# Transposed scores by query tile over four heads, three PSUM banks per kind of score, one visit per key tile to the values

## The chip, the cores and the metric

The kernel runs on one NeuronCore of a Trainium2 chip. The metric is the device time of one execution in microseconds, as the median of several runs. Engines are named as the profile names them: PE (TensorE, with its weight loads shown apart as PEld), DVE (VectorE), ACT (ScalarE), POOL (GpSimd) and SP (SyncE, which here only issues DMAs).

## The reference, cut to what matters

```python
x = L0_attn_x                                   # (2, 2048, 1024) float32
xn = layernorm(x)
q = (xn @ wq).reshape(b, s, 32, 32)             # 32 query heads of 32
k = (xn @ wk).reshape(b, s, 8, 32)              # 8 key heads, each serves 4 query heads
v = (xn @ wv).reshape(b, s, 8, 32)
scores = where(causal, q @ k.T / sqrt(32), min)
s = (softmax(scores) @ v).reshape(b, s, 1024) @ wo
base = xn @ W_base.T + b_base
g = silu(base + lora_out)                       # rank-16 experts, top 2 of 8 by a router
out = x + s * g
```

## The kernel before

The program has four stages that follow one another: `project` (layer norm, q, k, v, router), `attend`, `gate` (base and lora, silu) and `output` (wo and the residual). The change is in `attend`, and in the few constants that are made for it at the start of the program.

`attend` works on 16 groups (2 batches of 8 key heads). A group has four query heads that share one key head. Its 2048 queries are cut in 4 chunks of 512 (`c` = 0 to 3), and a chunk sees 4(c+1) key tiles of 128 keys (`j`). Four kinds of work run on PE, interleaved by a fixed order (`stage`), and the text calls them by the letters of that order:

- **S**, row scores (L747): for one query tile `i`, one head `h` and one piece of 512 keys `p`, queries lie on the partitions. DVE takes the maximum over the keys (L905). There are 160 pieces in a group, 64 of them on the diagonal, 128 to 512 keys wide, and each of these 64 gets a second matmul that adds a causal mask (L750). Four PSUM banks (`rows_ps`) hold them. The pieces are computed 72 ahead of T (`LEAD`), partly for the next group.
- **M**: when a chunk has all its maxima, `shift` is formed (L911), turned by PE (L756), copied by DVE (L915) and carried by a DMA into one more row of `q_st` (L675), so that T subtracts the maximum by itself.
- **T**, transposed scores (L804): for one key tile `j` and one head `h`, keys lie on the partitions and up to 512 queries on the columns. Two banks (`cols_ps`) hold them. On the diagonal a T is 512, 384, 256 or 128 wide and gets a mask matmul of 128 columns (L807). ACT takes the exponential into `probs`, one of four buffers, by key tile (L887). A group has 160 T, 64 of them on the diagonal.
- **V** (L821) and **L** (L831): the exponentials times the values, and times ones (the row sums), into `o_ps` and `l_ps`, four heads side by side in the columns of PE. V runs for all 40 key tiles of a group, L for 17. The exponentials of the other 23 are first added up by POOL (L737), 20 additions in a group, and one L for each of chunks 1 to 3 takes that sum at the chunk's end (**Y**, L841).

A step is one key tile: four T, each followed by one S. A V stands after the second pair and an L, where there is one, after the fourth. When a chunk is done, ACT copies `l_ps` and `o_ps` out (**O**, L896 and L897), DVE takes the reciprocal of the sums in eight slices of 128x64 between the S of the next chunk (L949), multiplies (L956), and SP stores the result. 14 of the 16 groups run in a loop whose body is two groups; it turns between chunk 0 and chunk 1.

## Time and profile before

| | |
|---|---|
| median of 3 runs | 3855.75 us (3852.77 to 3857.87) |
| span of the profiled execution | 3855.3 us |
| first S of `attend` on PE | 666.7 us |
| first T | 703.0 us |
| last matmul of `attend` | about 3078 us |
| first matmul of `gate` | 3094.9 us |
| mean granted TensorE clock | 0.981 of full speed |

From the first T to the last matmul of `attend` are 2375 us, 16 groups. The profile is read by stretches: a table of busy time by stretch gives what each engine does in one group, and the timeline of a few microseconds shows the matmuls with their start times. A matmul's duration contains its way through the array, so two that follow each other overlap in the records; what one costs PE is the distance from its start to the next start, not its duration. "Idle before" on PEld names what the weight load waited for.

### The profile page before, as it was taken

To read this page: it belongs to the slowest core of one execution; us is meant where nothing else is said; L and a number is where in the kernel's file an instruction comes from. 1 tells how busy PE (TensorE), PEld (TensorE's weight loads), DVE (VectorE), ACT (ScalarE), POOL (GpSimd) and SP (SyncE) were. 2 spreads that over 40 slices of the span, in tenths; PEclk is the share of its full clock that TensorE was granted. 3 is DMA by queue.
4 is the path that set the end of the run, shared out by engine and by line. 5 is a ranking of instruction groups with operands and counts; after the bars stand their busy time and mean duration, and the time that the engine had idled before them with its cause. 6 is when DMAs were issued, how large, how long until landed. Compare 5 with 4: busy or idle time off the path is not lost. (4 is left out here: it accounts for less than half of the span.)

```text
span 3855.3 us, 66009 instructions
## 1 busy us (share of the span) xinstructions
PE 3712.1 (96%) x21376; PEld 2272.1 (59%) x21376; DVE 2212.6 (57%) x4099; ACT 1557.0 (40%) x3042; POOL 1379.6 (36%) x349
## 2 busy tenths in 40 slices
PE   7999998999999999999999999999999889998999
PEld 6888886544444444444444444444444378887887
DVE  5343332877777777777777677777777322222333
ACT  3122210455555555555555555555555511011000
POOL 0000000465565574565465565555655600000000
PEclk9999998799999999999999999999999999999999
DMA  6555444211101102101101111111010054444555
GB/s 219 167 175 159 153 145 146 79 34 35 46 20 49 38 23 48 39 26 45 43 26 45 37 32 42 35 35 45 21 47 18 6 179 145 137 137 162 191 189 174
DMA packets 232906, 326.87 MB, mean 85 GB/s; under 512 B 16800, under 2 KB 132512, under 8 KB 231072
## 3 DMA queue, kind: packets, MB, share of 16 engines
q1 hardware_dynamic: 229008, 310.48, 26.7%
q10 hardware_dynamic: 3600, 12.58, 1.0%
q8 instruction: 167, 2.74, 0.3%
q14 instruction: 131, 1.07, 0.1%
HBM read 188.25 MB, written 134.22 MB: 84 GB/s over the span
## 5 line engine op out<-in xcount | busy, mean ns | idle before, releaser
L905 DVE TENSOR_REDUCE neg_max<-rows_ps 128x1 f32<-128x512 f32 (+3 forms) x2560 | 1434.3, 602 | 600.7 <-PE rows_ps L747 427.2
L887 ACT ACTIVATE probs<-cols_ps 128x512 f32<-128x512 f32 (+3 forms) x2560 | 1270.4, 533 | 1059.4 <-PE cols_ps L804 542.9
L737 POOL TENSOR_TENSOR added_pool<-added_pool,probs 128x2048 f32<-128x2048 f32 (+2 forms) x272 | 1137.0, 4180 | 296.6 <-ACT probs L887 285.5
L804 PE MATMUL cols_ps<-q_st,k_st 97*128 97x512 f32 (+3 forms) x2560 | 1089.6, 428 | 61.7 <-ACT probs L887 42.9
L747 PE MATMUL rows_ps<-k_st,q_st 96*128 96x512 f32 (+3 forms) x2560 | 1021.7, 405 | 16.9 <-DMA q_st<-scratch_q_hi 16.9
L804 PEld LDWEIGHTS cols_ps<-q_st,k_st 97*128 97x128 f32 x2560 | 488.2, 191 | 820.6 <-ACT probs L887 702.8
L821 PE MATMUL o_ps<-probs,v_st 128*32 128x512 f32 (+3 forms) x5120 | 605.7, 545 | 0.0
L747 PEld LDWEIGHTS rows_ps<-k_st,q_st 96*128 96x128 f32 x2560 | 510.6, 200 | 40.9 <-issue 17.1
L737 POOL TENSOR_TENSOR added_pool<-probs 128x2048 f32<-128x2048 f32 x48 | 219.5, 4573 | 726.3 <-ACT probs L887 726.3
L949 DVE RECIPROCAL l_raw<-l_raw 128x64 f32<-128x64 f32 x512 | 275.3, 540 | 56.2 <-ACT a_o_raw L897 56.2
L438 PE MATMUL acc<-xt_hi,w_hi 128*128 128x512 f32 x704 | 281.6, 400 | 0.6 <-DVE logits L381 0.6
L440 PE MATMUL acc<-xt_hi,w_lo 128*128 128x512 f32 x704 | 277.6, 394 | 0.0
L439 PE MATMUL acc<-xt_lo,w_hi 128*128 128x512 f32 x704 | 276.8, 393 | 0.0
L720 POOL TENSOR_TENSOR gw_lo<-gw_raw,gw_hi 128x1024 fp32r<-128x1024 f32 x9 | 21.0, 2372 | 672.3 <-ACT gw_hi L862 672.3
L750 PE MATMUL rows_ps<-mask_ij,ident_b 128*128 128x128 bf16 x1024 | 241.8, 236 | 0.0
L395 DVE SCALAR_TENSOR_TENSOR out_lo<-acc,out_hi 128x512 fp32r<-128x512 f32 x80 | 55.3, 692 | 324.4 <-ACT out_hi L290 324.4
L1082 PE MATMUL g_acc<-gw_hi,g_t_hi 128*128 128x512 f32 x576 | 225.2, 391 | 16.9 <-DMA g_t_lo<-scratch_hw_lo 16.9
L807 PE MATMUL cols_ps<-mask_ji,ident_b 128*128 128x128 bf16 x1024 | 237.9, 232 | 0.0
L831 PE MATMUL l_ps<-probs,ones 128*32 128x512 f32 (+3 forms) x2176 | 228.0, 491 | 0.0
L1083 PE MATMUL g_acc<-gw_lo,g_t_hi 128*128 128x512 f32 x576 | 224.9, 390 | 0.0
L1084 PE MATMUL g_acc<-gw_hi,g_t_lo 128*128 128x512 f32 x576 | 224.8, 390 | 0.0
L1202 PE MATMUL o_acc<-ow_hi,o_t_hi 128*128 128x512 f32 x512 | 200.4, 391 | 11.2 <-DVE o_t_lo L1168 11.2
(101 smaller groups left out, 3155.0 us busy)
## 6 DMA issues: line engine op xcount, KB each, us to landing
q_st<-scratch_q_hi SPq DMA_DIRECT2D x128, 256.0 KB, 4.4
x_sb<-in_x SPq DMA_DIRECT2D x32, 512.0 KB, 4.0
scratch_xt_hi<-xt_hi SPq DMA_DIRECT2D x32, 512.0 KB, 6.0
scratch_xt_lo<-xt_lo SPq DMA_DIRECT2D x32, 512.0 KB, 6.8
scratch_q_hi<-out_hi SPq DMA_DIRECT2D x64, 256.0 KB, 2.4
scratch_q_lo<-out_lo SPq DMA_DIRECT2D x64, 256.0 KB, 2.9
q_st<-scratch_q_lo SPq DMA_DIRECT2D x64, 256.0 KB, 4.6
scratch_o<-o_sb SPq DMA_DIRECT2D x64, 256.0 KB, 2.4
```

Source lines behind the costliest of these rows:

```text
L438: nc.tensor.matmul(out, lh, rh, start=(k == 0), stop=False)
L439: nc.tensor.matmul(out, lh, rl, start=False, stop=False)
L440: ins = nc.tensor.matmul(out, ll, rh, start=False, stop=(k == KT - 1))
L737: nc.gpsimd.tensor_tensor(added["pool"][:, :, q0:CH], a[:, :, q0:CH], probs[j % 4][:, :, q0:CH], ALU.add).then_inc(pool_added, 1)
L747: ins = nc.tensor.matmul(out[:, 0:keys], q_st[c][0:K1, h, i * P:(i + 1) * P], k_st[kbuf][0:K1, CH * p:CH * p + keys], start=True, stop=p < c)
L750: ins = nc.tensor.matmul(out[:, keys - P:keys], ident_b[:, :], mask_ij[:, :], start=False, stop=True)
L804: ins = nc.tensor.matmul(cols_ps[h % NCOLS][:, q0:CH], k_st[u][:, j * P:(j + 1) * P], q_st[c][:, h, q0:CH], start=True, stop=not diagonal)
L807: ins = nc.tensor.matmul(cols_ps[h % NCOLS][:, q0:q0 + P], ident_b[:, :], mask_ji[:, :], start=False, stop=True)
L821: ins = nc.tensor.matmul(o_ps[h * HD:(h + 1) * HD, q0:CH], v_st[vbuf][:, j, :], probs[j % 4][:, h, q0:CH], start=(j == 0), stop=(j == step ...
L887: nc.scalar.activation(probs[j % 4][:, h, q0:CH], cols_ps[h % NCOLS][:, q0:CH], ACT.Exp) \
L905: nc.vector.tensor_reduce(neg_max[chunk % 2][:, r, p:p + 1], rows_ps[bank % NROWS][:, 0:keys], AX.X, ALU.max, negate=True).then_inc(rows_f ...
L949: ins = nc.vector.reciprocal(l_raw[cp % 2][:, part], l_raw[cp % 2][:, part])
```

## The change

- **T by query tile.** One T is now one key tile `j` and one query tile `i` over all four heads: 4 x 128 = 512 columns, always. A group has 136 T, of which 16 are on the diagonal; each of these gets a mask matmul of 512 columns (`ident_r`, `mask_ji` in fp32r). ACT writes the exponentials of a T to four places of `probs`.
- **Banks.** Three `rows_ps` (were four), three `cols_ps` (were two); `probs` has five buffers (were four); `gw_raw` two (were four).
- **Row masks on DVE.** The 64 diagonal S of a group have no mask matmul. Their maximum is taken by `tensor_tensor_reduce`: the bank plus a constant `tri` in SBUF, written to `masked_rows` in bf16, with the maximum as accumulated result. In the program this is two DVE instructions, the second on 128x1.
- **One visit.** V and L of a key tile stand together (`weigh`), after the third T behind the key tile's last T. L runs for 16 key tiles, POOL makes 21 additions in a group. Y stands with the last visit of a chunk.
- **Order.** The S are spread evenly: 164 S and M over 136 T, 84 ahead. M comes after three S of the next chunk (was two). O stands two T behind a chunk's last visit.
- **Reciprocals.** The row sums are no longer inverted as 128x512. A DMA gathers one row of each head as 128x16 (L1), DVE inverts that in one instruction (I), a DMA stores it (L2), four DMAs read it back spread over the partitions (L3), DVE multiplies (N), a DMA stores the result (L4). I, L2, L3, N and L4 stand 8, 9, 13, 18 and 19 T behind the last visit of the chunk.
- The loop turns between chunks 1 and 2.

```diff
-LEAD = 72
-TURN_AFTER = 2
-NROWS, NCOLS = 4, 2
+TURN_AFTER = 3
+NROWS, NCOLS, NPROBS = 3, 3, 5
+LEAD = 84
+VISIT_AFTER = 3
+def tiles_of(c):
+    return [(j, i) for j in range(TPC * (c + 1)) for i in range(max(0, j - TPC * c), TPC)]
...
-ADDS = {"pool": [[], [0, 1, 3, 4, 6], [0, 1, 3, 4, 6, 7, 9, 10], [0, 1, 3, 4, 6, 7, 9, 10, 12, 13]]}
+ADDS = [[], [0, 1, 2, 4, 5], [0, 1, 2, 4, 5, 6, 8, 9], [0, 1, 2, 4, 5, 6, 8, 9, 10, 12, 13]]
...
+        _t = tiles_through(_c, _j) + VISIT_AFTER - 1
+        event(_t, "W", _c, _j)
+    event(_t + 2, "O", _c)
+    event(_t + 4, "L1", _c)
+    event(_t + 8, "I", _c)
+    event(_t + 9, "L2", _c)
+    event(_t + 13, "L3", _c)
+    event(_t + 18, "N", _c)
+    event(_t + 19, "L4", _c)
...
-                if p == c:
-                    ins = nc.tensor.matmul(out[:, keys - P:keys], ident_b[:, :], mask_ij[:, :], start=False, stop=True)
...
+                keys = keys_of(c, i, p)
+                wait_apart(dve, rows_full, full, passed_rows)
+                nc.vector.tensor_tensor_reduce(masked_rows[rows_slot(k)][:, 0:keys], bank[:, 0:keys], tri[:, CH - keys:CH],
+                                               1.0, MASKED, ALU.add, ALU.max, into).then_inc(rows_free, 1)
...
-                        ins = nc.tensor.matmul(cols_ps[h % NCOLS][:, q0:CH], k_st[u][:, j * P:(j + 1) * P], q_st[c][:, h, q0:CH],
-                                               start=True, stop=not diagonal)
+                        ins = nc.tensor.matmul(into, k_st[n.u][:, j * P:(j + 1) * P], q_st[c][:, :, i * P:(i + 1) * P],
+                                               start=True, stop=not diagonal)
+                        if diagonal:
+                            ins = nc.tensor.matmul(into, ident_r[:, :], mask_ji[:, :, :], start=False, stop=True)
...
-                        ins = nc.vector.reciprocal(l_raw[cp % 2][:, part], l_raw[cp % 2][:, part])
+                        nc.vector.reciprocal(l_inv[cc % 2][:, :], l_few[cc % 2][:, :]).then_inc(l_inv_ready, 1)
```

First place, PE in chunk 3, key tiles below the diagonal (`cols_ps` is T, `rows_ps` is S or M, `o_ps` is V, `l_ps` is L or Y). Before, from one T to behind the next V:

```order
L804 MATMUL cols_ps0<-q_st3,k_st0 128x512
L747 MATMUL rows_ps3<-k_st1,q_st1 128x512
L804 MATMUL cols_ps1<-q_st3,k_st0 128x512
L747 MATMUL rows_ps0<-k_st1,q_st1 128x128
L750 MATMUL rows_ps0<-mask_ij,ident_b 128x128
L804 MATMUL cols_ps0<-q_st3,k_st0 128x512
L747 MATMUL rows_ps1<-k_st1,q_st1 128x512
L821 MATMUL o_ps<-probs1,v_st0 32x512 x4
```

The same place now, with the last visit of chunk 2 in it:

```order
L895 MATMUL cols_ps2<-q_st3,k_st0 128x512
L818 MATMUL rows_ps1<-k_st1,q_st0 128x512
L855 MATMUL o_ps<-probs3,v_st0 32x128 x4
L860 MATMUL l_ps<-probs3,ones 32x128 x4
L867 MATMUL l_ps<-added,ones 32x512 x4
L895 MATMUL cols_ps0<-q_st3,k_st0 128x512
L818 MATMUL rows_ps2<-k_st1,q_st1 128x512
L895 MATMUL cols_ps1<-q_st3,k_st0 128x512
L818 MATMUL rows_ps0<-k_st1,q_st1 128x128
L818 MATMUL rows_ps1<-k_st1,q_st1 128x512
L895 MATMUL cols_ps2<-q_st3,k_st0 128x512
L824 MATMUL rows_ps2<-ident,shift 16x128
```

The T rotate over three banks, an S has no mask behind it, some T are followed by two S, and V, L and Y stand in one block.

Second place, PE on the diagonal of chunk 1. Before:

```order
L831 MATMUL l_ps<-probs2,ones 32x512 x4
L804 MATMUL cols_ps0<-q_st1,k_st1 128x384
L807 MATMUL cols_ps0<-mask_ji,ident_b 128x128
L747 MATMUL rows_ps3<-k_st1,q_st3 128x512
L804 MATMUL cols_ps1<-q_st1,k_st1 128x384
L807 MATMUL cols_ps1<-mask_ji,ident_b 128x128
L747 MATMUL rows_ps0<-k_st1,q_st3 128x512
L821 MATMUL o_ps<-probs3,v_st1 32x512 x4
```

Now:

```order
L895 MATMUL cols_ps0<-q_st1,k_st1 128x512
L898 MATMUL cols_ps0<-mask_ji,ident_r 128x512
L818 MATMUL rows_ps0<-k_st1,q_st3 128x512
L895 MATMUL cols_ps1<-q_st1,k_st1 128x512
L818 MATMUL rows_ps1<-k_st1,q_st3 128x512
L895 MATMUL cols_ps2<-q_st1,k_st1 128x512
L818 MATMUL rows_ps2<-k_st1,q_st3 128x512
L855 MATMUL o_ps<-probs3,v_st1 32x512 x4
```

Where each narrow T had a mask, one full T in a key tile has one.

Third place, DVE at the end of a chunk's normalisation (`rows_ps` into `neg_max` or `row_max` is the maximum of an S). Before:

```order
L905 TENSOR_REDUCE neg_max1<-rows_ps1 128x1
L905 TENSOR_REDUCE neg_max1<-rows_ps2 128x1
L949 RECIPROCAL l_raw0<-l_raw0 128x64
L905 TENSOR_REDUCE neg_max1<-rows_ps3 128x1
L905 TENSOR_REDUCE neg_max1<-rows_ps0 128x1
L949 RECIPROCAL l_raw0<-l_raw0 128x64
L956 TENSOR_TENSOR o_sb0<-a_o_raw0,l_raw0 128x512
```

Now, in chunk 1, where the N of the group before's chunk 3 meets the I of chunk 0:

```order
L960 TENSOR_REDUCE row_max1<-rows_ps0 128x1
L1007 RECIPROCAL l_inv0<-l_few0 128x16
L1011 TENSOR_TENSOR o_sb1<-o_sb1,l_all1 128x512
L960 TENSOR_REDUCE row_max1<-rows_ps1 128x1
L960 TENSOR_REDUCE row_max1<-rows_ps2 128x1
L964 ISA masked_rows0,row_max1<-rows_ps0,tri 128x128
L964 ISA row_max1 128x1
```

Eight slices became one small instruction, a diagonal maximum became two instructions, and the multiplication comes earlier in the chunk than before.

## Rows read from the trace of the kernel before

**Rows 1.** The page, part 1 (PE) and part 2 (granted clock).

```profile
PE 3712.1 (96%) x21376; PEld 2272.1 (59%) x21376; DVE 2212.6 (57%) x4099; ACT 1557.0 (40%) x3042; POOL 1379.6 (36%) x349
...
PEclk9999998799999999999999999999999999999999
```

**Rows 2.** Busy time by stretch, two stretches of one group; columns in the first line.

```profile
core 0: us, PE busy (x) PEld busy (x) DVE busy (x) ACT busy (x) POOL busy (x), PEclk, DMA share, GB/s
...
1440.60:1587.60 147.00, 143.95 (x936) 69.45 (x932) 109.80 (x204) 82.60 (x168) 84.81 (x21) 1.00 0.15 37
1587.62:1739.52 151.90, 146.65 (x937) 70.72 (x933) 109.96 (x204) 82.93 (x168) 84.77 (x21) 0.98 0.14 36
```

**Rows 3.** Timeline of PE in chunk 3: start, duration, work, [idle before].

```profile
1700.48 0.50 PE L804 MATMUL cols_ps<-q_st,k_st 97*128 97x512 f32 x1
...
1701.66 0.19 PEld L804 LDWEIGHTS cols_ps<-q_st,k_st 97*128 97x128 f32 x1 [0.21 <-ACT probs L887]
...
1703.77 0.50 PE L804 MATMUL cols_ps<-q_st,k_st 97*128 97x512 f32 x1
...
1704.10 0.40 PE L747 MATMUL rows_ps<-k_st,q_st 96*128 96x512 f32 x1
...
1704.34 0.40 PE L804 MATMUL cols_ps<-q_st,k_st 97*128 97x512 f32 x1
...
1704.58 0.28 PE L747 MATMUL rows_ps<-k_st,q_st 96*128 96x256 f32 x1
...
1704.71 0.23 PE L750 MATMUL rows_ps<-mask_ij,ident_b 128*128 128x128 bf16 x1
...
1704.87 1.07 PE L831 MATMUL l_ps<-probs,ones 128*32 128x512 f32 x8
...
1705.86 0.19 PEld L804 LDWEIGHTS cols_ps<-q_st,k_st 97*128 97x128 f32 x1 [0.84 <-ACT probs L887]
```

**Rows 4.** Timeline around the copies of O.

```profile
1468.91 0.60 ACT L897 ACTIVATE a_o_raw<-o_ps 128x512 f32<-128x512 f32 x1
...
1470.06 0.50 PE L804 MATMUL cols_ps<-q_st,k_st 97*128 97x512 f32 x1 [0.67 <-ACT probs L887]
```

**Rows 5.** Groups by line and form, 800 to 3000 us: count, busy us, mean ns.

```profile
L905 DVE TENSOR_REDUCE neg_max<-rows_ps 128x1 f32<-128x512 f32 x1664 | 1081.4, 681 | 455.4 <-PE rows_ps L747 405.3 <-PE rows_ps L750 34.3 <-issue 5.4
...
L737 POOL TENSOR_TENSOR added_pool<-added_pool,probs 128x2048 f32<-128x2048 f32 x193 | 882.1, 4571 | 211.4 <-ACT probs L887 203.9
...
L949 DVE RECIPROCAL l_raw<-l_raw 128x64 f32<-128x64 f32 x479 | 259.3, 541 | 0.0
```

**Rows 6.** Timeline of DVE and POOL where a multiplication meets an addition.

```profile
1506.39 9.24 POOL L737 TENSOR_TENSOR added_pool<-added_pool,probs 128x2048 f32<-128x2048 f32 x2 [2.11 <-ACT probs L887]
...
1514.62 1.56 DVE L956 TENSOR_TENSOR o_sb<-a_o_raw,l_raw 128x512 f32<-128x512 f32 x1
```

**Rows 7.** Timeline of the diagonal: an S behind a T's mask.

```profile
1606.28 0.48 PE L747 MATMUL rows_ps<-k_st,q_st 96*128 96x512 f32 x1
...
1606.60 0.22 PE L804 MATMUL cols_ps<-q_st,k_st 97*128 97x128 f32 x1
...
1606.70 0.47 PE L747 MATMUL rows_ps<-k_st,q_st 96*128 96x512 f32 x1
```

**Rows 8.** Timeline where the loop turns.

```profile
1612.10 0.79 PE L804 MATMUL cols_ps<-q_st,k_st 97*128 97x512 f32 x1 [2.19 <-issue]
```

**Rows 9.** Timeline: first S of `attend`, first matmul of `gate`.

```profile
666.71 0.45 PE L747 MATMUL rows_ps<-k_st,q_st 96*128 96x128 f32 x1 [16.93 <-DMA q_st<-scratch_q_hi]
...
3094.86 0.79 PE L1082 MATMUL g_acc<-gw_hi,g_t_hi 128*128 128x512 f32 x1 [16.87 <-DMA g_t_lo<-scratch_hw_lo]
```

**Rows 10.** One line's instructions (T): count, ns min/median/max, first and last start.

```profile
L804 PE MATMUL cols_ps<-q_st,k_st x2560: 223/421/796, 703.0 to 3075.3; 97*128 97x512 f32 x139, 97*128 97x384 f32 x20, 97*128 97x128 f32 x19, 97*128 97x256 f32 x19
```

**Rows 11.** The page: a DVE form that reads a bank and SBUF.

```profile
L395 DVE SCALAR_TENSOR_TENSOR out_lo<-acc,out_hi 128x512 fp32r<-128x512 f32 x80 | 55.3, 692 | 324.4 <-ACT out_hi L290 324.4
```

**Rows 12.** DMA issues: the shortest, median us to landing.

```profile
q_st<-row SPq DMA_DIRECT2D x64, 8.0 KB, 1.8
```

More of the change, by code:

```diff
@@ new lines, with tiles_through, cols_slot, before_in @@
+NSG = len(ROWS)
+TILES = [(c, j, i) for c in range(CPB) for j, i in tiles_of(c)]
+NTG = len(TILES)
+T_OFF = [sum(len(tiles_of(cc)) for cc in range(c)) for c in range(CPB + 1)]
+J_OFF = [TPC * c * (c + 1) // 2 for c in range(CPB + 1)]
+NJG = J_OFF[CPB]
+NVG = NJG
+LEAD = 84
+VISIT_AFTER = 3
+assert NJG % NPROBS == 0
+def tiles_through(c, j):
+    return T_OFF[c] + sum(1 for t in tiles_of(c) if t[0] <= j)
+def cols_slot(t):
+    return 1 if t == NTG - 1 else t % NCOLS
+def before_in(slot_of, count, t):
+    return next(p for p in range(t - 1, -count, -1) if slot_of(p % count) == slot_of(t))
@@ L542, in stage @@
     return order
 STAGES = [stage(c) for c in range(CPB)]
-def before(op):
-    return op[0] in ("O", "I", "N") or op[-1] == "before"
-def first_uses():
-    out = []
-    for i in range(LEAD):
-        out.append(("S", *piece_at(i)))
-        if i >= TURN_AFTER and piece_at(i - TURN_AFTER)[2]:
-            out.append(("M", *piece_at(i - TURN_AFTER)[:2]))
-    return out
-FIRST_USES = first_uses()
-USES = [sum(op[0] in "SM" for op in st) for st in STAGES]
-NSG = sum(USES)
-S_OFF = [len(FIRST_USES) + sum(USES[:c]) for c in range(CPB)]
@@ L566, with of_group_before, of_group_after @@
[L566 to L581 removed]
+def of_group_before(op):
+    return op[0] not in "TSM" and op[2] == 1
+def of_group_after(op):
+    return op[0] in "SM" and op[3] == 1
@@ L583, in attend, with adds_through @@
+FIRST_ROWS = [k for k in range(LEAD) if ROWS[k] != ("M", CPB - 1)]
+ADDS = [[], [0, 1, 2, 4, 5], [0, 1, 2, 4, 5, 6, 8, 9], [0, 1, 2, 4, 5, 6, 8, 9, 10, 12, 13]]
+NADD = sum(len(a) - 1 for a in ADDS if a)
+def adds_through(c, j):
+    return sum(max(0, len(a) - 1) for a in ADDS[:c]) + sum(1 for t in ADDS[c][1:] if t <= j)
+def attend(nc, sc, ident, ident_r, mask_ji, tri, wb, lb, gw_hi, gw_lo):
     ctx = ExitStack()
@@ L774, in run @@
+            def run(n, c, ops):
                 for op in ops:
                     kind = op[0]
-                    if kind in "VLY":
-                        old = op[-1] == "before"
-                        cc = (c - 1) % CPB if old else c
-                        back = 1 if old and c == 0 else 0
-                        steps = TPC * (cc + 1)
-                        to_sum = [j for j in range(steps) if not any(j in ADDS[who][cc] for who in ADDS)]
-                        adders = [who for who in ADDS if ADDS[who][cc]]
@@ L920, in _ @@
             ins.then_inc(ones_ready, 1)
[L921 to L933 removed]
+            dve.sem_inc(rows_free, 1)
@@ L934, in run @@
+            for k in FIRST_ROWS:
+                count = rows_count(None, 0, k)
+                if ROWS[k][0] == "S":
+                    _, chunk, last, piece = ROWS[k]
+                    piece_max(count, k, chunk, *piece)
+                    if last:
+                        shifts(chunk, count)
+                else:
+                    row_out(count, k, ROWS[k][1] % 2)
+            def run(n, c, ops):
                 for op in ops:
                     kind = op[0]
-                    at = S_OFF[c] + use
```

506 lines of the change are left out of this document (263 added, 243 removed).

## Prediction

> **What bounds the kernel now.** I read the page first: PE is busy 96% of the span, at nearly full granted clock, and no other engine is over 57% [rows 1]. A busy PE may still be waiting, because a matmul's record holds its way through the array, so I went on to the stretches. A group of `attend` takes 147.0 us, and there DVE is busy 109.8, ACT 82.6 and POOL 84.8 us; none of them sets the pace by its sum [rows 2]. Then the timeline of PE. At the 2.4 GHz level a full S or T starts 0.24 us after the one before it (1704.10, 1704.34, 1704.58). A V or L takes 0.99 us until the next T's start (1704.87 to 1705.86), and the S behind that T comes after 0.33 us instead of 0.24, because the T's weight load was not hidden. Two T and two S with a block take 2.09 us (1703.77 to 1705.86), all of it PE's own work. Two T and two S without a block take 1.18 us (1700.48 to 1701.66), and 0.21 of these are a wait for ACT, which has not emptied the second bank [rows 3]. Behind the two copies of O the next T waits 0.67 us and the step loses about 1.25 us [rows 4]. So PE's own work is about 137 of the 147 us, and ACT's banks cost the other 10. That work, and then the waits, are where the change acts. `project`, `gate` and `output` keep their code.
>
> **The change part by part**, in us for each group.
>
> T and their masks. Both kernels stream 136 x 512 columns for T, but before in 160 starts and 64 masks. An S behind a mask takes 0.32 instead of 0.24, and a 128 wide T with its mask takes 0.10 on top (1606.28, 1606.60, 1606.70) [rows 7]; a mask therefore costs about 0.12. The 64 diagonal T average 0.16, so with masks 64 x 0.28 = 17.9. Now 40 full T and 16 full masks at 0.24: 13.4. Some narrow T hide their load better than I assume; I take -3.5, bounds -1 and -5.
>
> Row masks leave PE. Where an S stands before a V or L, the mask is absorbed: 1704.58 to 1704.71 to 1704.87 is hardly more than the array needs to drain. Elsewhere it costs the 0.12 of above. About a third of the S stand before a block: 64 x 0.08 = -5, bounds 0 and -8.
>
> One visit. Of 17 L, 6 already stood right behind a V. The other 11 each cost an entry and an exit: 0.99 less the 0.85 of four passes over 512 columns is 0.14, then 0.09 for the exposed load and some 0.14 to drain the S before it, 0.37 in all: -4. The L now cover 896 columns fewer in four passes, -1.5. Together -5.5.
>
> Bank waits on T. 80 pairs of T less 51 blocks and the 4 with O leave 25 halves at 0.21: -5. With three banks and 136 exponentials of 0.55 to 0.6 (80 us in a group) ACT has no deficit to hand on: by the time a visit starts, the exponential it needs has been waited for by a T. O: the copies stand two T behind a visit and take 1.2; V of the next chunk's first tile stands two T later, about 1.0 us, and needs them. The T behind wait about 0.75 where they waited 1.25: 4 x -0.5 = -2.
>
> DVE. 96 plain maxima go back to back at 0.55 to 0.6, as now. The diagonal ones are a form that the trace lacks; the nearest row, one bank and one SBUF input, takes 0.69 for 512 [rows 11], where the plain one takes 0.68 [rows 5], so 0.49 for the mean width of 320, and the second instruction adds about 0.15. Reciprocals shrink from 32 x 0.54 = 17 [rows 5] to 4 small ones. The sum is 96 x 0.57 + 64 x 0.64 + about 10 = 106 of some 132: not the bound, but with three banks instead of four its bursts now reach PE. The Trainium skill gives such a two-input fp32 operation (N + 151) / 0.96 ns ("VectorE: DVE Perf Modes", The TRN2 errata), 0.49 us for 320; by that page the sum stays as it is.
>
> The multiplication N has both inputs in SBUF, and the trace shows what it does beside POOL: it starts at 1514.62, POOL's addition ends at 1515.63, and it ends at 1516.18, 0.55 later [rows 6]. It waits for the whole addition. In the new order N of chunk 3 falls 10 T into chunk 1, about 7.5 us in, inside POOL's first addition (about 6.5 to 11.1). DVE is away some 4 us, PE has three banks of S, about 2 us: a stall of 2. The other three fall near an addition's end, 0.5 together. The chain of I needs the copies plus one DMA of about 1.8 [rows 12], 5 us; 6 T and two visits lie between, so it just arrives. Adding 0.08 for each of 40 visits for the third bank I take +6, bounds 0 and +16.
>
> POOL. 18 full and 3 narrower additions are 18 x 4.57 + 3 x 3.45 = 93 [rows 5]. They begin when a chunk's second tile is ready, and Y waits for the last. In chunk 3 that is 6.5 + 44.6 + 1.8 (a gap before tile 4) = 53, where Y stands at about 53 too. Over the group this floor is about 125. So POOL's cover of Y is just used up; any further gain on PE would end there.
>
> Sum: 147 - 3.5 - 5 - 5.5 - 5 - 2 + 6 = 132 us for a group, -15; over 16 groups -240.
>
> Once per run. The turns of the loop cost about 5 us each, 2.19 of it at the first T [rows 8], and stay. The distance from the first T to the last, 2372 [rows 10], is 16 x 147 + 7 x 5 less 15, part of which the last group owes to having no S; now POOL holds that group back, +5. Before the first T stand 36 us of S (666.7 to 703.0) [rows 9, 10]; 9 more S and one bank fewer, at the 1.2 GHz level, +10. The loading of `gate`'s weights through two buffers ends before that. At the end four DMA hops of about 2 replace 3.5 us of reciprocals: +6. Constants at the start: +2. Together +23.
>
> 3855.3 - 240 + 23 = 3638 as a span. The median of the runs shown is 0.45 above the profiled span, so 3639.
>
> **The rivals.**
>
> POOL's floor (A). If masks and blocks were worth their upper bounds and DVE did not disturb, PE alone would need about 121, and Y would hold the group at 125: 3855 - 352 + 23 = 3526. For it: PE in the profile has no other releaser than ACT. Against: three `rows_ps` and a loaded DVE.
>
> DVE as bound (B). If the new form runs at two cycles an element, a diagonal maximum costs 1.0 instead of 0.64 and DVE needs 96 x 0.57 + 64 x 1.0 + 10 = 129, in bursts; a group ends at about 139: 3855 - 128 + 23 = 3750. For it: the form is not in the trace and is two instructions. Against: [rows 11].
>
> Slower (C): the diagonal maximum waits for POOL as N does. It reads `tri` from SBUF, 64 times a group, while POOL is busy 93 us. A wait that meets POOL at random costs half an addition, 2.3 us, in a share 93/G of the cases: G = 132 + 64 x 2.3 x 93/G gives G = 200, so 3855 + 53 x 16 + 23 = 4726. It decides from about 0.25 us of unhidden wait for each diagonal maximum. For it: [rows 6] show the lock with certainty, for two SBUF inputs. Against: in the new form one input is a bank; no row has such a form while POOL works. The Trainium skill says a DVE instruction with at most one SBUF input outside the two-port modes does not contend with GpSimd ("SBUF — State Buffer", Who interferes with whom). By that rule C is out and 3639 stands, without it the time is that of C; the lock on N, by the same section, agrees with the trace.
>
> Nothing gained (D): the long matmul masks, the fetch of the longer DVE program or a late DMA in the chain L1 to L3 (N would hold DVE, then PE) eat the 15 us, about 3.8 us in each chunk: 3855 + 23, with the additions once per run, 3878 at the point where all is eaten. For it: SP's queue holds L3 of one chunk before L1 of the next, and DVE stands in order at I and N. Against: the distances above, which leave some 4 us for each hop of about 2.
>
> **How the numbers follow.** The forecast, 3560 to 3720, has 0.63; A 0.11; B 0.15; C 0.05; D 0.06, most of it slower. The range takes in A and B with their own widths: 3525 to 3790. The bounds of the terms give 147 - 1 - 0 - 5.5 - 5 - 2 + 16 = 149 on one side if all fall badly at once, and POOL's floor on the other; I take no more than half of the bad side. A measurement of this kernel can tell about 0.2% from no change. Faster 0.89, within 0.2% 0.01, slower 0.10.
>
> **What would show it.** In the profile after: a group of about 132 us between two turns of the loop; PEld of T no longer waiting for ACT except behind O; new waits of PE for DVE (`row_max`), the longest beside the multiplication of chunk 3; ISA records of the diagonal maxima of about 0.49 plus 0.15; Y waiting little or not for POOL; POOL busy about 93 of 132. If the diagonal maxima show durations of up to an addition, it is C. If DVE is busy over 95% of a group, it is B. If Y waits for POOL in each chunk, it is A. Waits for a DMA at the reciprocal or the multiplication mean D.

## The result: 3913 us, slower by 1.5%

The changed kernel takes 3913.16 us (median of 4 runs, 3910.23 to 3920.0), the kernel before 3856.69 beside it. The ratio is 1.0149, with a 95% interval of 1.0135 to 1.0163. The forecast was 3639, range 3525 to 3790: sign and range were both wrong.

The page of the changed kernel, part 1, and from part 2 the row of the granted clock:

```profile
PE 3604.7 (92%) x19072; PEld 2230.1 (57%) x19072; DVE 2143.2 (55%) x4677; ACT 1491.2 (38%) x2658; POOL 1527.9 (39%) x366
...
PEclk9999998898999899999999989999999989999999
```

Beside [rows 1] PE has 107 us less work in a span that is 53 us longer, and the clock is no longer at 9 in every slice of `attend`. A group, from one Y of chunk 2 to the same Y of the next group, and the next one, which has a turn of the loop in it; the columns are those of [rows 2]:

```profile
1407.16:1557.01 149.85, 136.91 (x796) 66.86 (x789) 105.69 (x241) 78.58 (x144) 93.98 (x21) 0.94 0.17 45
1557.01:1710.89 153.88, 139.83 (x797) 67.94 (x789) 105.53 (x241) 78.99 (x144) 93.97 (x21) 0.92 0.17 43
```

So a group takes 149.85 us where the forecast said 132. PE is busy for 136.9 of them, but part of that time at a lower clock (0.94 in the mean). Part 5 of the page, two of the rows that differ most from before: S (L818) and the multiplication N (L1011).

```profile
L818 PE MATMUL rows_ps<-k_st,q_st 96*128 96x512 f32 (+3 forms) x2560 | 987.1, 410 | 182.9 <-DVE row_max L960 118.2
...
L1011 DVE TENSOR_TENSOR o_sb<-o_sb,l_all 128x512 f32<-128x512 f32 x64 | 234.2, 3659 | 10.0 <-DMA l_all<-scratch_l_inv 10.0
```

N is an instruction of 0.69 us when nothing disturbs it, and takes 3659 ns on average here. In the kernel before, S waited for no maximum. Now PE is idle for 182.9 us in front of it, 118.2 of them until a maximum (L960) has freed a bank. The waits between 900 and 2700 us (engine, line, releaser: us in total, times, longest):

```profile
PEld cols_ps L895 <- ACT probs L939: 231.0, 304, 1.2
...
PE rows_ps L818 <- DVE row_max L960: 85.6, 36, 3.0
...
PE rows_ps L818 <- DVE row_max L964: 33.8, 12, 2.8
...
PEld l_ps L867 <- POOL added L801: 0.3, 2, 0.2
```

PE waits 119.4 us for DVE in 48 stalls of 2.5 us each: four in each group, one for each N. Y hardly waits for POOL (0.3 us), and T's weight loads wait 231 us for ACT where they waited 528.3 with two banks.

**Where N stands.** The timeline of DVE and POOL in one group, the rows of N in chunk 1 and of the additions next to them:

```profile
1484.20 4.56 POOL L801 TENSOR_TENSOR added<-probs 128x2048 f32<-128x2048 f32 x1 [19.23 <-ACT probs L939]
...
1486.89 2.43 DVE L1011 TENSOR_TENSOR o_sb<-o_sb,l_all 128x512 f32<-128x512 f32 x1
...
1488.85 4.88 POOL L801 TENSOR_TENSOR added<-added,probs 128x2048 f32<-128x2048 f32 x1
...
1497.34 8.41 POOL L801 TENSOR_TENSOR added<-added,probs 128x2048 f32<-128x2048 f32 x2 [3.61 <-ACT probs L939]
...
1498.37 4.07 DVE L1011 TENSOR_TENSOR o_sb<-o_sb,l_all 128x512 f32<-128x512 f32 x1
```

The first N starts 2.69 us into an addition and ends 0.56 us behind its end (1489.32 less 1488.76), as in [rows 6]. The second starts 1.0 us into an addition, waits for the rest of it, and takes 4.07. The N of the next two chunks start at 1529.74 and 1574.51, 0.7 and 1.2 us behind the start of an addition (1529.01, 1573.34), and take 4.37 and 3.92.

**What PE does meanwhile.** Its timeline at the second N: an S of chunk 1 finds all three banks full, waits, and what follows is slower.

```profile
1497.66 0.40 PE L818 MATMUL rows_ps<-k_st,q_st 96*128 96x512 f32 x1
1497.90 0.40 PE L895 MATMUL cols_ps<-q_st,k_st 97*128 97x512 f32 x1
...
1503.09 0.79 PE L818 MATMUL rows_ps<-k_st,q_st 96*128 96x512 f32 x1 [2.79 <-DVE row_max L960]
1503.68 0.63 PE L895 MATMUL cols_ps<-q_st,k_st 97*128 97x512 f32 x1
1504.11 0.63 PE L818 MATMUL rows_ps<-k_st,q_st 96*128 96x512 f32 x1
```

Ahead of the stall two full matmuls start 0.24 us apart, behind it 0.43. That is the 1.2 GHz level. Busy time in the 7 us behind each of the four stalls of this group, from the stall's end (the granted clock is the third number from the right):

```profile
1429.11:1436.11 7.00, 7.00 (x24) 3.25 (x24) 5.07 (x13) 3.38 (x7) 5.18 (x2) 0.76 0.10 39
...
1489.97:1496.97 7.00, 6.90 (x40) 3.30 (x40) 4.38 (x11) 2.57 (x5) 3.76 (x1) 1.00 0.24 76
...
1503.09:1510.09 7.00, 7.00 (x34) 3.50 (x34) 4.03 (x9) 2.35 (x4) 2.66 (x1) 0.54 0.43 114
...
1534.76:1541.76 7.00, 6.99 (x22) 3.58 (x22) 4.56 (x10) 2.73 (x5) 4.18 (x2) 0.61 0.10 37
```

In this group three of the four stalls are followed by a spell at a lower granted clock. What a spell costs is estimated as its length times what is missing to 1.00: 1.7, 0, 3.2 and 2.7 us, 7.6 together. The stalls themselves are 2.81, 1.73, 2.79 and 2.96 us, 10.3. Both together are 17.9 us a group, and the question for the experiments is whether a group without them takes 149.9 - 17.9 = 132.0.

One group is not enough to price a stall. Between 900 and 2700 us all 35 stalls of 2.77 to 2.98 us are followed by a lower clock, with means of 0.50 to 0.76 over the next 7 us, 2.6 us lost on average. Of the 11 stalls of 1.73 to 1.75 us seven are followed by one (0.65 to 0.76) and four are not; that is 1.1 us lost on average. The same stall one group later:

```profile
1640.38:1647.38 7.00, 6.90 (x31) 3.46 (x35) 4.32 (x10) 2.39 (x4) 3.74 (x1) 0.76 0.22 77
```

### The profile page after: what moved, and what is told of

Its sections match the earlier page's. It is cut to its first block and busy times, and to the rows that moved or that the text cites. A ratio compares the mean times of both kernels' runs of the same rounds, so it can differ in the third digit from the quotient of the medians.

```text
span 3908.4 us, 62660 instructions
## 1 busy us (share of the span) xinstructions
PE 3604.7 (92%) x19072; PEld 2230.1 (57%) x19072; DVE 2143.2 (55%) x4677; ACT 1491.2 (38%) x2658; POOL 1527.9 (39%) x366
## 5 line engine op out<-in xcount | busy, mean ns | idle before, releaser
L939 ACT ACTIVATE probs<-cols_ps 128x512 f32<-128x512 f32 x2176 | 1204.4, 599 | 1148.2 <-PE cols_ps L895 978.5
L801 POOL TENSOR_TENSOR added<-added,probs 128x2048 f32<-128x2048 f32 (+1 forms) x288 | 1283.4, 4456 | 306.5 <-ACT probs L939 290.9
L960 DVE TENSOR_REDUCE row_max<-rows_ps 128x1 f32<-128x512 f32 x1536 | 1010.8, 685 | 370.2 <-PE rows_ps L818 365.3
L818 PE MATMUL rows_ps<-k_st,q_st 96*128 96x512 f32 (+3 forms) x2560 | 987.1, 410 | 182.9 <-DVE row_max L960 118.2
L895 PE MATMUL cols_ps<-q_st,k_st 97*128 97x512 f32 x2176 | 967.2, 454 | 12.6 <-issue 7.2
L895 PEld LDWEIGHTS cols_ps<-q_st,k_st 97*128 97x128 f32 x2176 | 431.3, 199 | 603.8 <-ACT probs L939 318.7
L818 PEld LDWEIGHTS rows_ps<-k_st,q_st 96*128 96x128 f32 x2560 | 519.4, 203 | 434.0 <-DVE row_max L960 258.3
L964 DVE CUSTOM_DVE_ANT_0 masked_rows<-rows_ps,tri 128x128 bf16<-128x128 f32 (+3 forms) x1024 | 490.2, 485 | 338.8 <-PE rows_ps L818 335.9
L855 PE MATMUL o_ps<-probs,v_st 128*32 128x512 f32 (+3 forms) x5120 | 642.2, 575 | 34.0 <-ACT o_sb L950 31.6
L801 POOL TENSOR_TENSOR added<-probs 128x2048 f32<-128x2048 f32 x48 | 219.7, 4578 | 601.5 <-ACT probs L939 601.5
L1011 DVE TENSOR_TENSOR o_sb<-o_sb,l_all 128x512 f32<-128x512 f32 x64 | 234.2, 3659 | 10.0 <-DMA l_all<-scratch_l_inv 10.0
L855 PEld LDWEIGHTS o_ps<-probs,v_st 128*32 128x32 f32 x5120 | 104.5, 111 | 233.5 <-ACT probs L939 102.1
```

The lines of the kernel that those rows point to most:

```text
L801: nc.gpsimd.tensor_tensor(added[:, :, q0:CH], other[:, :, q0:CH], probs_of(c, j)[:, :, q0:CH], ALU.add).then_inc(pool_added, 1)
L818: nc.tensor.matmul(rows_ps[rows_slot(k)][:, 0:keys], q_st[c][0:K1, h, i * P:(i + 1) * P], k_st[kbuf][0:K1, CH * p:CH * p + keys], start=Tr ...
L855: ins = nc.tensor.matmul(o_ps[h * HD:(h + 1) * HD, q0:CH], v_st[vbuf][:, j, :], probs_of(cc, j)[:, h, q0:CH], start=(j == 0), stop=(j == s ...
L895: ins = nc.tensor.matmul(into, k_st[n.u][:, j * P:(j + 1) * P], q_st[c][:, :, i * P:(i + 1) * P], start=True, stop=not diagonal)
L939: nc.scalar.activation(probs_of(c, j)[:, :, i * P:(i + 1) * P], cols_ps[cols_slot(t)][:, :].rearrange("p (h q) -> p h q", h=NREP), ACT.Exp) \
L960: nc.vector.tensor_reduce(into, bank[:, :], AX.X, ALU.max).then_inc(rows_free, 1)
```

## The experiments

The time of every run below is the median of 4 runs; ratios are to the kernel before on the same chip.

**Without the lock.** N is replaced by an instruction with one small input; the output is then not divided by the row sums.

```diff
-nc.vector.tensor_mul(o_sb[cc % 2][:, :], o_sb[cc % 2][:, :], l_all[cc % 2][:, :]).then_inc(norm_ready, 1)
+nc.vector.reciprocal(l_few[cc % 2][:, :], l_few[cc % 2][:, :]).then_inc(norm_ready, 1)
```

> The changed kernel with the multiplication N (L1011, two SBUF inputs) replaced by a small one-input instruction on 128x16, so the output is not divided by the row sums. All else stays: the DMAs, the order, the banks. Theory 1 (the lock and the clock): in the changed kernel N waits for POOL's addition, holds DVE for 3.7 us in the mean, four times in a group; PE runs out of its three banks, waits about 10 us in a group, and then works at 1.2 GHz for a while (mean clock 0.93 in a group, so about 21 us at half speed, 10 lost). Both go: a group falls from 149.9 to about 130, the run to about 3590, the clock in a group to 0.99 or more. Rival 2 (PE's own work is longer than worked out: exposed loads, two S in a row, long masks): a group stays over 143 and the run over 3800. Rival 3 (only the wait goes, the clock falls for another reason): about 140 and 3750 with the clock still near 0.93.

Measured: 3636.48 us (3632.65 to 3637.57), ratio 0.9433 [0.9418, 0.9449]. Busy time by stretch, one group and the next with its loop turn:

```profile
1383.60:1515.12 131.52, 129.05 (x796) 64.30 (x792) 91.37 (x241) 78.22 (x145) 92.92 (x21) 1.00 0.20 50
1515.12:1652.09 136.97, 131.16 (x797) 65.12 (x793) 91.53 (x241) 78.28 (x145) 92.83 (x21) 0.99 0.19 48
```

A group is 131.52 us at full clock, near the 132.0 of the sum above (the expectation had said about 130, and 3590 for the run), and PE waits 0.3 us for DVE in 1800. The four multiplications are the whole 277 us between this and the changed kernel, though four undisturbed ones need only 4 x 0.69 us of an engine that is idle for 40 of the 131.5.

**N on POOL.** A complete kernel: the multiplication stands in POOL's own order, so that nobody waits for a lock.

```diff
+elif op[0] == "N":
+    cc, back = op[1:3]
+    wait_apart(pool, l_spread[cc % 2], ..., passed_pool)
+    nc.gpsimd.tensor_tensor(o_sb[cc % 2][:, :], o_sb[cc % 2][:, :], l_all[cc % 2][:, :], ALU.mult).then_inc(norm_ready, 1)
```

> The changed kernel with the multiplication N moved from DVE to POOL, at the same place of the order; complete computation. Theory 1: DVE is never held, so as e1; POOL gets 4 x about 1.2 us more in a group (93 to 98) and its chain of additions up to Y is the next bound: a group of 129 to 134, the run 3600 to 3680. Rival 2: over 3800, as in e1. A third outcome would be that POOL waits for the spread sums in front of an addition and Y waits for POOL: then Y's weight load shows POOL as releaser for some us in each chunk and the run ends between.

Measured: 3657.47 us (3656.56 to 3660.51), ratio 0.949 [0.9474, 0.9506]. POOL's timeline in chunk 1:

```profile
1404.66 4.57 POOL L802 TENSOR_TENSOR added<-probs 128x2048 f32<-128x2048 f32 x1 [18.71 <-ACT probs L946]
1409.19 1.28 POOL L814 TENSOR_TENSOR o_sb<-o_sb,l_all 128x512 f32<-128x512 f32 x1
1410.43 4.57 POOL L802 TENSOR_TENSOR added<-added,probs 128x2048 f32<-128x2048 f32 x1
```

And PE's waits for POOL between 900 and 2700 us:

```profile
PE l_ps L874 <- POOL added L802: 15.0, 21, 0.8
```

POOL needs 1.28 us for what DVE does in 0.69, and still the kernel is 256 us faster than with N on DVE. What it pays over the run without the lock, 21 us, is mostly Y's wait for POOL: 0.7 to 0.8 us at chunk 2's Y in every group and 0.7 at chunk 1's in every other one, 1.1 us a group and 18 in all. (The next expectation puts all of it on chunk 1; the trace does not.)

**N on POOL, two T earlier.** L3, N and L4 at 12, 16 and 17 T behind the last visit.

```diff
-event(_t + 13, "L3", _c)
-event(_t + 18, "N", _c)
-event(_t + 19, "L4", _c)
+event(_t + 12, "L3", _c)
+event(_t + 16, "N", _c)
+event(_t + 17, "L4", _c)
```

> The changed kernel with N on POOL, and L3, N and L4 one, two and two T earlier (12, 16 and 17 behind the last visit). In the version with N on POOL at its old place only the Y of chunk 1 waits for POOL, 0.8 us in each group, because two multiplications of 1.28 stand between chunk 1's additions. Two T earlier the multiplication of chunk 3 should fall before chunk 1's first addition, in POOL's idle time: the wait at Y goes down by 0.6 or more, 3640 to 3655. Rival: POOL is then behind at the DMA (L3 lands later than N's place) and the additions start late: 3657 to 3690.

Measured: 3660.17 us (3657.43 to 3663.57), not told apart from the version above, 5 us above the range of the first theory and inside the rival's. The waits between 900 and 2700 us:

```profile
POOL o_sb L814 <- DMA l_all<-scratch_l_inv: 27.1, 13, 2.3
...
PE l_ps L874 <- POOL added L802: 13.9, 7, 2.2
```

POOL waits 2.1 us in each group for a row sum that is still on its way. Y waits less often and longer, 13.9 us instead of 15.0. The gain that was expected did not come: POOL stood at the DMA instead, as the rival had it, but at no cost either.

**The additions split by head.** Four POOL instructions of 128x512 in place of one of 128x2048: the lock is as frequent, and shorter.

```diff
-nc.gpsimd.tensor_tensor(added[:, :, q0:CH], other[:, :, q0:CH], probs_of(c, j)[:, :, q0:CH], ALU.add).then_inc(pool_added, 1)
+for h in range(NREP):
+    ins = nc.gpsimd.tensor_tensor(added[:, h, q0:CH], other[:, h, q0:CH], probs_of(c, j)[:, h, q0:CH], ALU.add)
+ins.then_inc(pool_added, 1)
```

> The changed kernel with every POOL addition cut into four, one for each head (128x512 instead of 128x2048). N stays on DVE. Theory 1: N waits for at most one short addition, so it takes 0.7 to 1.9 us instead of 2.4 to 4.4, and PE's waits behind it vanish within the three banks; by the trace 1024 columns take 2.37 us and 2048 take 4.57, so a quarter takes about 1.3 and POOL's sum grows from 93 to about 103 in a group: a group of 131 to 138, the run 3610 to 3720, with Y waiting for POOL at the upper end. If the lock is held over a whole chain of additions rather than one instruction, N stays near 4 us and the run near 3910.

Measured: 3772.49 us (3766.97 to 3773.16), ratio 0.9785 [0.9769, 0.9802]. The instructions of the tile `o_sb` (count, duration in ns min/median/max, first and last start):

```profile
L1012 DVE TENSOR_TENSOR o_sb<-o_sb,l_all x64: 680/920/1801, 744.9 to 2998.7; 128x512 f32<-128x512 f32 x64
```

The waits of PE between 900 and 2700 us:

```profile
PE l_ps L868 <- POOL added L802: 53.2, 31, 2.1
...
PE rows_ps L819 <- DVE row_max L961: 11.5, 14, 0.9
```

N never takes more than 1.8 us now, PE waits 11.5 us for DVE instead of 119.4, and 141 us come back. It still is 52 us above the expected range. POOL is busier (1319 of these 1800 us, against 1255 in the faster kernel without the lock), and Y pays with 53 us.

**N two T earlier and two T later, on DVE.** Two kernels that change only where N stands.

```diff
-event(_t + 18, "N", _c)
-event(_t + 19, "L4", _c)
+event(_t + 20, "N", _c)
+event(_t + 21, "L4", _c)
```

and the other with L3, N and L4 at 12, 16 and 17.

> The changed kernel, complete computation, with only places in the order moved: N stands 16 T behind a chunk's last visit (was 18), L3 12 (was 13), L4 17 (was 19). In e1 the place of N was 0.7 to 1.2 us behind the start of an addition that follows 1 to 2 us of idle POOL; two T earlier (1.1 to 1.6 us) is in that idle time. Theory 1 (N's wait for the addition, and PE's stall and clock behind it): N takes 0.7 to 1.3 us in most cases, a group about 132 to 134, the run 3630 to 3690, although nothing else is changed. Rival (N's length does not matter, or its input comes by the DMAs too late): the run stays over 3850; a late DMA would show as N waiting for l_all.

> The changed kernel with N 20 T behind the last visit (was 18) and L4 21. N then starts some 1.6 to 2.3 us later within the same addition, so it waits that much less: 2.0 to 2.5 us in the mean instead of 3.7. Theory 1: PE's three banks cover nearly all of it, little low clock, the run 3680 to 3780. Rival: no effect, 3910.

Measured: earlier 3713.45 us (3711.7 to 3717.7), ratio 0.9632 [0.9615, 0.9648]; later 3771.77 us (3760.88 to 3778.64), ratio 0.9775 [0.9757, 0.9793]. The tile `o_sb` of the earlier and of the later one:

```profile
L1011 DVE TENSOR_TENSOR o_sb<-o_sb,l_all x64: 680/820/4399, 741.1 to 2944.9; 128x512 f32<-128x512 f32 x64
```

```profile
L1011 DVE TENSOR_TENSOR o_sb<-o_sb,l_all x64: 692/2613/2911, 745.2 to 3005.9; 128x512 f32<-128x512 f32 x64
```

The place of one instruction, two T to either side, is worth 140 to 200 us. The place of 18 T is the worst of the three: there all four N of a group meet an addition, three of them at its start. Two T earlier three of the four take 0.7 to 1.8 us, but chunk 3's now takes 3.4 to 4.4 and stalls PE for 2.98 each time; that is why this run ended 23 us above its expected range. Two T later the time was as expected and the reason given for it was not: PE still stalls for 1.4 to 1.9 us at three of the four N (62.5 us in 1800), and the run's clock is 0.959.

**DVE away for as long, without a lock.** In place of N a reciprocal of one SBUF input, 512 or 256 wide; it meets no lock and is long by itself. Again nothing is normalised.

```diff
-nc.vector.tensor_mul(o_sb[cc % 2][:, :], o_sb[cc % 2][:, :], l_all[cc % 2][:, :]).then_inc(norm_ready, 1)
+nc.vector.reciprocal(o_sb[cc % 2][:, 0:512], l_all[cc % 2][:, 0:512]).then_inc(norm_ready, 1)
```

> The changed kernel; in place of the multiplication N, DVE makes a reciprocal of 128x512 from `l_all` into `o_sb`: one SBUF input instead of two, but long by itself. The output is not normalised. From the 64 and the 16 wide reciprocals of the profiles (0.541 and 0.247 us) I estimate 3.3 us, close to the 3.66 that N takes when it waits for POOL. Theory (what costs is that DVE is away for so long, and that the TensorE clock falls after PE's stall, whoever keeps DVE away): PE waits about 2.1 us at each, 8 in a group, the granted clock of `attend` is 0.93 to 0.95, time 3845 to 3895. Rival (it is the lock with POOL that hurts, also in other ways than by DVE's absence; without it four long operations are hidden by the banks): 3636 to 3700, clock 0.99.

> As the run with the 128x512 reciprocal, but 128x256, an estimated 1.7 us, and again not normalised. Theory: three banks of S cover about 1.2 us of DVE's absence (3.66 less the 2.5 that PE waits for each N in the changed kernel), so PE waits 0.5 at each, 2 in a group, and a stall so short costs little clock: 3665 to 3710, clock of `attend` 0.98. If cost grew in proportion to DVE's absence with no cover, it would be (1.7 - 0.25) / (3.66 - 0.25) of the 277 us between the changed kernel and the one without the lock, 118, so 3754.

Measured: 512 wide 3923.88 us (3912.98 to 3928.48), ratio 1.0165 [1.0147, 1.0183]; 256 wide 3706.14 us (3702.15 to 3712.89), ratio 0.9611 [0.9595, 0.9628]. The groups by form and then the waits, 900 to 2700 us, of the 512 wide one:

```profile
L1011 DVE RECIPROCAL o_sb<-l_all 128x512 f32<-128x512 f32 x46 | 153.3, 3332 | 0.0
```

```profile
PE rows_ps L818 <- DVE row_max L960: 73.8, 35, 2.9
...
PE rows_ps L818 <- DVE row_max L964: 26.1, 12, 2.2
```

The same of the 256 wide one:

```profile
L1011 DVE RECIPROCAL o_sb<-l_all 128x256 f32<-128x256 f32 x52 | 90.0, 1732 | 0.0
```

```profile
PE rows_ps L818 <- DVE row_max L960: 22.5, 40, 1.3
...
PE rows_ps L818 <- DVE row_max L964: 7.5, 13, 0.6
```

No lock, 3.33 us of DVE in place of 3.66, and the time is as bad. So DVE's absence alone is enough for the whole loss, and no other effect of the lock is needed. With 1.73 us the damage is 70 us instead of 287: it isn't proportional, since the banks cover about the first microsecond (the trace shows stalls of 0.57 and 0.9 to 1.3 us) and less is lost behind stalls this short. Behind 10 of the 13 of 0.92 us and more the clock stays at 1.00 over the next 7 us, behind the other three it is 0.53, 0.54 and 0.76 (estimated over the run, from 0.975 against 0.979: 15 of the 70 us). Rows of this kernel's PE behind a stall of 0.94 us that is followed by no lower clock (the last two starts are 0.24 us apart):

```profile
1428.66 1.09 PE L818 MATMUL rows_ps<-k_st,q_st 96*128 96x512 f32 x2 [0.94 <-DVE row_max L960]
...
1431.02 0.40 PE L818 MATMUL rows_ps<-k_st,q_st 96*128 96x512 f32 x1
1431.25 0.40 PE L895 MATMUL cols_ps<-q_st,k_st 97*128 97x512 f32 x1
```

The 512 wide one came out 29 us above its range. PE's wait was near the expected 8 us a group (99.9 us in 1800, 8.7 a group), but the clock of the whole run was lower than in the changed kernel, 0.937 against 0.946. Part of this can be read: at three places of a group its stalls are shorter than the changed kernel's (1.88 to 2.19 us instead of 2.8 to 3.0), and still a lower clock follows 33 of these 35. At the fourth, chunk 3's, where N had stalled PE for 1.73, they are longer, 2.53 to 2.91, and a lower clock follows all 11, with 2.8 us lost on average instead of 1.1. The 7 us behind one of them:

```profile
1641.05:1648.05 7.00, 6.91 (x19) 3.39 (x19) 3.67 (x9) 2.00 (x4) 2.47 (x1) 0.53 0.22 77
```

Over its four places the 7 us behind the stalls lose 9.7 us a group, where the changed kernel's lose 8.9. The two clocks differ by more, an estimated 2.2 us a group (0.009 of 3920 us); the rest stays open.

**Four banks for S, two for T.** The changed kernel with the numbers of banks of before.

```diff
-NROWS, NCOLS, NPROBS = 3, 3, 5
+NROWS, NCOLS, NPROBS = 4, 2, 5
```

> The changed kernel with four banks for S and two for T (was three and three). N keeps its lock of 3.7 us. Theory 1: one more S, 0.7 us, is covered each time, so PE's stalls shrink by some 3 us in a group and the low clock with them; but T waits for its second bank again, 5 us in a group by the prediction's term: 3850 to 3930. Rival (the third T bank is worth nothing): 3800 or less.

Measured: 3912.98 us (3902.03 to 3916.95), ratio 1.0144 [1.0124, 1.0163]: the same time. The waits between 900 and 2700 us:

```profile
PEld cols_ps L895 <- ACT probs L939: 425.5, 832, 1.2
...
PE rows_ps L818 <- DVE row_max L960: 61.1, 35, 2.4
...
PE rows_ps L818 <- DVE row_max L964: 25.6, 12, 2.1
```

A fourth bank takes 0.6 us from each stall (86.7 us for 47, so 1.8 each) and raises the run's clock from 0.946 to 0.958, together about 90 us by the prices of the table below. The time is the same, so something gives those 90 us back. T with two banks is the likely taker, as its loads wait 425.5 us where they waited 231.0, but no run shows T's third bank alone. The expectation held in its number, by effects that cancel. And a fourth bank for S does not hide N: stalls of 1.8 us remain.

**The row masks back on PE.** The changed kernel with the mask matmul of before on each diagonal S.

```diff
+                if p == c:
+                    ins = nc.tensor.matmul(rows_ps[rows_slot(k)][:, keys - P:keys], ident_b[:, :], mask_ij[:, :], start=False, stop=True)
...
-                nc.vector.tensor_tensor_reduce(masked_rows[rows_slot(k)][:, 0:keys], bank[:, 0:keys], tri[:, CH - keys:CH],
-                                               1.0, MASKED, ALU.add, ALU.max, into).then_inc(rows_free, 1)
+                nc.vector.tensor_reduce(into, bank[:, 0:keys_of(c, i, p)], AX.X, ALU.max).then_inc(rows_free, 1)
```

> The changed kernel with the row masks put back on PE (a 128 column mask matmul in bf16 behind each of the 64 diagonal S of a group) and a plain maximum on DVE for all S. The lock of N stays. By the prediction's term this costs 5 us in a group (bounds 0 to 8): about 155, the run about 3990. Rival: the diagonal maxima in two DVE instructions with a wait of their own are what starves PE; then the run is at or under 3910.

Measured: 3967.56 us (3964.84 to 3976.06), 54 us above the changed kernel, 3.4 a group. PE's wait for DVE is nearly what it was (114.9 us in 1800, in 46 stalls), so most of the difference is the masks'.

**The same part alone, in the kernel before.** Diagonal maxima by `tensor_tensor_reduce`, no row masks on PE, all else as before.

```diff
-                if p == c:
-                    ins = nc.tensor.matmul(out[:, keys - P:keys], ident_b[:, :], mask_ij[:, :], start=False, stop=True)
...
+                nc.vector.tensor_tensor_reduce(masked_rows[bank % NROWS][:, 0:keys], rows_ps[bank % NROWS][:, 0:keys],
+                                               tri[:, CH - keys:CH], 1.0, MASKED, ALU.add, ALU.max, into).then_inc(rows_free, 1)
```

> The kernel before with one part of the change alone: no mask matmul for the row scores, the diagonal maximum by `tensor_tensor_reduce` with `tri` in SBUF. Theory: PE is what bounds, and masks that leave it give 3.4 us in a group as they cost when they were put back, so 3856 - 54 = 3802, range 3785 to 3825. Rival: with two `cols_ps` a PE that has less to do between two T only meets ACT sooner (528 us of weight loads wait for ACT already), and the time stays within 10 us of 3857.

Measured: 3815.65 us (3812.55 to 3818.09), ratio 0.9891 [0.9875, 0.9908]: 40 us, 2.5 a group. The difference to 3.4 is likely what the rival said, in part: T's loads wait 619.7 us for ACT between 900 and 2700 us where it was 528.3, since two banks empty no faster for it.

**The kernel before, N one key tile later.** Does the lock hurt there too?

```diff
-        if j == (3 if c == 0 else 5):
+        if j == (3 if c == 0 else 6):
```

> The kernel before with its multiplication (L956) one key tile later in chunks 1 to 3, which puts two of the four in a group 0.6 us behind the start of an addition: they should take about 4.4 us instead of 1.6 to 1.7. Theory 1: the kernel before has four banks of S and sends one S each 0.84 us, so it covers about 3.4 us: PE stalls by 1 us or less each time and the clock stays up: 3860 to 3900. If the lock costs 5 us each time whatever the banks, it is 3855 + 2 x 5 x 16 = 4015.

Measured: 3964.58 us (3945.72 to 3974.02), ratio 1.0293 [1.0275, 1.031]. The tile `o_sb` in the kernel before, then in this one, and then this one's waits between 900 and 2700 us:

```profile
L956 DVE TENSOR_TENSOR o_sb<-a_o_raw,l_raw x64: 691/1369/2641, 745.4 to 3082.6; 128x512 f32<-128x512 f32 x64
```

```profile
L956 DVE TENSOR_TENSOR o_sb<-a_o_raw,l_raw x64: 691/2716/5055, 748.2 to 3171.3; 128x512 f32<-128x512 f32 x64
```

```profile
PE rows_ps L747 <- DVE neg_max L905: 36.0, 24, 1.6
```

The kernel before has the same lock at a harmless place: its N take 0.69 to 2.6 us, and PE's S never wait for them. One key tile later two of the four in a group take 4.9 and 5.1 us, and the kernel loses 109 us, 65 more than the top of the expected range. With four banks PE stalls for 1.4 to 1.6 us, not for 1 or less, and the clock did not stay up. The profiled run is the fastest of the four (3945.72): its span is 89 us longer than before, of which the waits explain 49 and the clock (0.973 against 0.981) 32. The other three took 3964 to 3974 us with clocks of 0.965 to 0.968.

**The sum over the runs.** Two prices should give every time, as an estimate: the wait of PE for DVE and POOL (the rows above, taken for 1800 us and scaled to the length of `attend`), and the clock, as the span times what the mean granted clock of the profiled run lacks to the 0.979 of the run without the lock.

| kernel | N, median ns | PE waits in 1800 us | clock | sum, us | measured, us |
|---|---|---|---|---|---|
| no lock | - | 0 | 0.979 | 3636 | 3636 |
| N on POOL | 1274 | 15.0 | 0.978 | 3658 | 3657 |
| N on POOL, earlier | 1280 (mean) | 13.9 | 0.977 | 3660 | 3660 |
| one input, 256 | 1732 (mean) | 30.0 | 0.975 | 3688 | 3706 |
| N two T earlier | 820 | 39.0 | 0.967 | 3729 | 3713 |
| additions split | 920 | 64.7 | 0.967 | 3762 | 3772 |
| N two T later | 2613 | 62.5 | 0.959 | 3790 | 3772 |
| as changed | 3986 | 119.4 | 0.946 | 3924 | 3913 |
| one input, 512 | 3332 (mean) | 99.9 | 0.937 | 3935 | 3924 |

For the changed kernel: 3636 + 119.4 x 2403/1800 + 3908 x 0.033 = 3636 + 159 + 129. That is 11 us too much; the seven other kernels come out within 18 us, over a spread of 287 us. By this estimate about 45% of the loss is clock. The kernel with four and two banks is not in the table: by the same prices it would take 3834 us, 79 less than it did, which is the open place named there.

## Why the prediction was wrong

**The step that failed is N**, in the term "DVE", +6 with bounds 0 and +16. Three things were wrong in it.

- Where N falls. For chunk 3's N the working was right: inside POOL's first addition, a stall of 2 us (measured 1.73). It was expected to be the longest of the waits and is the shortest. "The other three fall near an addition's end, 0.5 together" was not worked out in the same way, and was false. They start 0.7 to 1.2 us into an addition and stall PE for 2.81, 2.79 and 2.96 us, 8.6 together. The mechanism was known from [rows 6]; it was worked out for one of four places.
- What a stall costs. I counted the wait alone. Behind each stall of 2.8 to 3.0 us PE runs at the 1.2 GHz level for a while, which costs another 2.6 us on average. This was no term of the sum and no rival. The trace of before had the price, and I had the row in hand: at the turn of the loop PE stands still for 2.19 us and the first T behind it takes 0.79 [rows 8]. I took "about 5 us" for a turn and left unasked why it is more than the 2.19. Two stretches of the kernel before, ahead of this turn and behind it:

```profile
1602.00:1610.00 8.00, 7.91 (x59) 3.44 (x57) 7.29 (x16) 2.66 (x9) 0.00 (x0) 1.00 0.69 162
1612.10:1620.00 7.90, 7.90 (x47) 4.13 (x47) 3.14 (x5) 3.09 (x6) 0.00 (x0) 0.62 0.11 38
```

7.9 us at 0.62 are 3.0 us lost, as much as behind the stalls of the changed kernel. 2.19 + 3.0 is the "about 5". The kernel before has six such pauses between 900 and 2700 us, and a lower clock follows five of them.
- The bound. The term went up to +16, and the range then took no more than half of the bad side. The four N alone cost 10.3 us of waiting and 7.6 of clock in the group above, 17.9, where the term had 2.5 for them; that is above the bound for all of DVE.

**What stood.** Without N's lock the kernel takes 3636 us and a group 131.5, where the prediction had 3639 and 132. That they are so near is luck: 2.5 us for N stood in the 132. With them taken out its sum was 129.5, so the other terms together were 2 us too good, and the run would have been forecast at 3599. The row masks are the one term that was tested alone: 3.4 us a group, not 5. The terms for T by query tile, for one visit, for T's third bank and for O have no run of their own. One sign of theirs did not come: T's loads still wait for ACT, 395 times in 1800 us without the lock, some 30 in each group, and not only behind O. Three banks of S in place of four were given 3.2 us, and without the lock cost nothing that PE shows (0.3 us in 1800). The once-per-run terms came out at about +28 instead of +23 (3635.8 less 3855.3 - 16 x 15.5, in the run without the lock): in the changed kernel the first T is at 711.1 instead of 703.0 (predicted +10, and +2 for constants, of which the first S shows 1.0), and the last Y waits 6.86 us for POOL (predicted +5).

**The rivals.** A, POOL's floor: not reached, Y waits 0.3 us in 1800. B, DVE as bound: DVE is busy 91 of 131.5 us without the lock. C, the slower side, had the right mechanism at the wrong instruction: it asked whether the diagonal maximum waits for POOL. It doesn't; the longest of them takes 0.69 us. The forms by width, 800 to 3000 us, while POOL is busy 62% of the time:

```profile
L964 DVE CUSTOM_DVE_ANT_0 masked_rows<-rows_ps,tri 128x512 bf16<-128x512 f32 x232 | 158.1, 686 | 98.8 <-PE rows_ps L818 98.8
...
L964 DVE DVE_READ_ACCUMULATOR2_ANT row_max<- 128x1 f32 x928 | 76.2, 82 | 0.0
...
L964 DVE CUSTOM_DVE_ANT_0 masked_rows<-rows_ps,tri 128x128 bf16<-128x128 f32 x232 | 65.6, 283 | 35.2 <-PE rows_ps L818 33.6
```

With one bank and one SBUF input the means are 283 to 686 ns, with no sign of a 4.6 us addition in them, and the pair costs 0.57 us on average where 0.64 was forecast; with two SBUF inputs N's mean is 3659. The Trainium skill draws the line at the same place ("SBUF — State Buffer", Who interferes with whom). It also says of the port pair that DVE and GpSimd share that whoever starts first has it for the whole instruction (same page, SBUF: two separate sides), and N's rows agree: the first N above ends 0.56 us behind the end of the addition that it met. The Trainium skill's formula for an fp32 `tensor_tensor` addition ("VectorE: DVE Perf Modes", The TRN2 errata) gives, as an estimate for this form, 291 and 691 ns for 128 and 512 columns, and these rows agree within 3%. D, nothing gained by masks, fetches or late DMAs: N waited 10.0 us for its DMA in the whole run, and that was not the cause.

So the rival that was missing is N itself at all four of its places. It could have been priced before: the order shows at which T each N and each addition stands, [rows 6] show what a meeting costs, and C's own arithmetic, an addition's length times how often it is met, had only to be applied to four instructions.
